# Eight-layer post-norm network on one core: weights requested a layer ahead, merged blocks around the 4-bit layer and the group norm, four-slot projections

## The chip, the core and the metric

The kernel runs on one core of a Trainium2 chip. The core has five engines with a queue of instructions each: TensorE (PE: matmuls, with PEld for its weight loads), VectorE (DVE), ScalarE (ACT), GpSimd (POOL) and SyncE (SP, which here only issues DMA transfers). They meet through semaphores. The metric is the time of one execution on the device in microseconds (us), the median of several.

## The reference

A batch of 1024 tokens with 256 features passes eight layers. After each layer the input is added and the sum is normalised (no scale or shift):

```
x = layernorm(x + linear_attention(x))        # 16 heads of 16
x = layernorm(x + golden_experts(x))          # 8 experts, 2 of them with low-rank additions
x = layernorm(x + grouped_attention(x))       # gqa: 16 query heads of 128, 4 groups
x = layernorm(x + top8_of_32_experts(x))
x = layernorm(x + latent_attention(x))        # mla: low-rank q, k, v, rotary part
x = layernorm(x + four_bit_ffn(x))            # q4
x = layernorm(x + differential_attention(x))  # diff: 16 heads of 128
x = layernorm(x + ternary_ffn(x))             # tern: weights rounded to -1, 0, 1
```

The two layers whose arithmetic the change rearranges:

```
dequant4bit(q, scale) = (q.astype(float32) - 7.5) * repeat(scale, 64, axis=1)
four_bit_ffn:  w_up = dequant4bit(w_up_q, w_up_scale).T
  y1 = x @ w_up + b_up + x @ up_lora_a @ up_lora_b;  x2 = relu(y1)
  y2 = x2 @ w_down + b_down + x2 @ down_lora_a @ down_lora_b
differential_attention, after the heads:
  out = (out - mu) * rsqrt(var + eps)               # over the 128 features of a head
  out = (out * gw + gb) * (1 - 0.8);  return out.reshape(b, s, 2048) @ Wo
```

## The kernel before

**Precision and products.** A float32 product is made of three fp32r matmuls: each operand is split in a high part (ACT copies it with rounding) and a low part (operand minus high part), and `product3` (lines L99, L100, L101) adds hi*hi, lo*hi and hi*lo. The activations are split once per layer into `x_hi` and `x_lo` by the closing of the layer before; weights are split where they are used, the low part often on POOL.

**Blocks.** A layer consists of one or two blocks. In a block each engine has its own program, in the order in which it is written; nothing is scheduled. At a block's end all engines meet in a barrier, so nothing of the next block, its DMA requests on SP among it, begins earlier. There is no work in flight across the boundary.

**`finish_layer`** (fin0, fin2, fin4, fin5, fin6, fin7, by the layer's number) projects an attention's or feed-forward's result back to 256 features and closes the layer. The contraction has `nk` chunks of 128 (2, 16, 2, 8, 16, 6), for eight tiles of 128 tokens. For a chunk ACT makes `h_hi` (128x1024, L289) and then `w_hi` (128x256, L291), DVE makes `h_lo` (L278), POOL makes `w_lo` (L266), and PE runs 8 tiles x 3 matmuls of 256 columns. There are two slots for the four split tiles, and the middle chunks run in a hardware loop (`in_pairs`); a slot is free again when PE signals `used`. The last two chunks are run tile by tile, so that the accumulators are finished one after the other. In fin7 the weights are exact in one part, and a chunk is 8 x 2 matmuls (L237, L238). Then `Closing` runs: DVE adds the residual (L139) and takes statistics, ACT takes the root, both normalise half of the tiles each, PE transposes (L200, 16), and ACT and DVE make `x_hi` and `x_lo`.

**The starts of the layers.** The first block of each layer lets SP request all its weights. golden requests the router, `temperature` and `before`, then experts and twelve low-rank pieces; gqa requests group 0, and POOL splits it (L1086, L1089) before PE may begin; mla requests 13 pieces (L1505 is the first PE use) while DVE clears the zero-padded `v_pad` (L1683, L1686) ahead of its copies L1691 and L1693 of PE's transposed weights; diff requests heads 0 and 1, then the lambda vectors and the group norm's rows, and POOL splits (L1961, L1963); tern requests `w1` to `w3`, and DVE sums `w1` (L2396).

**q4** dequantises both weights on DVE (centre L1813, scale L1816), then PE makes `up` in four parts (per part one matmul of 16x512 at L1838 and four at L1840; the trace has two records for each) and `down` in four (L1848, L1850), adding the low-rank product; 16 jobs of six matmuls of 512 columns (unit of 128 features x half of the tokens) follow. POOL adds `b_down` to `x_tok` (L1805).

**diff_norm** is a block after diff: statistics, then per head six tiles are normalised on DVE (L2290) and two on ACT (L2324), PE transposes them (L2308), and ACT applies the norm's weight and bias while it copies them to `feat` (L2335). fin6 follows with 16 chunks.

## Time and profile before

| | us |
|---|---|
| median of 3 runs (lowest to highest) | 1868.95 (1864.26 to 1869.68) |
| the profiled execution | 1871.95 |
| its span, first to last instruction | 1870.2 |
| PE busy (9441 matmuls) | 1581.6, 85% |
| DVE, ACT, POOL busy | 1041.8, 878.2, 395.5 |
| mean granted TensorE clock | 0.915 |

A matmul's busy time in the trace is longer than its distance to the next one, because matmuls are pipelined; costs are read from start to start. A row of the timeline gives the start, the duration, the engine, the line, what is written and read, and in brackets how long the engine had been idle and what ended it. DVE 56%, ACT 47% and POOL 21% are averages over stages that differ.

### The profile page before, as it was taken

What the parts mean: (1) busy time and instruction counts of PE and PEld (TensorE: products, weight loads), DVE (VectorE), ACT (ScalarE), POOL (GpSimd) and SP (SyncE); (2) the same over time, 40 slices, a digit from 0 to 9 for tenths busy, and PEclk for the clock granted to TensorE, in tenths of its full rate; (3) what the DMA queues carried; (4) which work ended last, traced back from release to release, by engine and by line L of the source; (5) the groups of instructions that cost most, each with busy time, mean ns of one, the idle gap of its engine ahead of it and who ended that gap; (6) DMA issues with size and microseconds to landing.
All of it is one profiled execution on the core that took longest, in us unless ns stands there. A gap on an engine that the chain in (4) does not pass through costs nothing. (4 is left out here: it accounts for less than half of the span.)

```text
span 1870.2 us, 27151 instructions
## 1 busy us (share of the span) xinstructions
PE 1581.6 (85%) x9441; PEld 1288.6 (69%) x9441; DVE 1041.8 (56%) x2034; ACT 878.2 (47%) x1895; POOL 395.5 (21%) x377
## 2 busy tenths in 40 slices
PE   7589959999989789995688669679999999985866
PEld 6468846766769668884466446658888888874855
DVE  3554535365363534445477640457877888766354
ACT  3343324444453333333466413346666666658433
POOL 0034531011004054542735000301101100000400
PEclk9789979999999799997799867899999999988968
DMA  1151120000000353311345020000000000001010
GB/s 55 40 154 46 46 62 18 17 0 17 0 0 0 105 136 102 90 46 30 55 59 65 5 52 0 21 13 15 18 17 8 17 17 8 9 1 45 0 47 23
DMA packets 76092, 68.12 MB, mean 36 GB/s; under 512 B 32176, under 2 KB 67208, under 8 KB 76016
## 3 DMA queue, kind: packets, MB, share of 16 engines
q1 hardware_dynamic: 71312, 62.73, 12.6%
q0 software_dynamic: 4704, 4.40, 1.9%
q8 instruction: 44, 0.72, 0.2%
q14 instruction: 32, 0.26, 0.0%
HBM read 56.46 MB, written 1.21 MB: 31 GB/s over the span
## 5 line engine op out<-in xcount | busy, mean ns | idle before, releaser
L2115 ACT ACTIVATE diff_att_probs<-psum,diff_att_neg_max 128x512 f32<-128x512 f32 x256 | 174.7, 697 | 26.9 <-DVE diff_att_neg_max L2177 26.9
L2177 DVE TENSOR_REDUCE diff_att_neg_max<-psum 128x2 f32<-128x1024 f32 x128 | 153.1, 1217 | 24.3 <-PE psum L2015 24.3
L99 PE MATMUL psum<-fin_w_hi,fin_h_hi 128*128 128x256 f32 x352 | 108.7, 309 | 45.2 <-POOL fin_w_lo L266 45.2
L2036 PE MATMUL psum<-diff_att_v_tok,diff_att_mixed_t 128*128 128x128 f32 x1024 | 127.5, 279 | 0.8 <-ACT diff_att_mixed_t L2121 0.8
L2036 PEld LDWEIGHTS psum<-diff_att_v_tok,diff_att_mixed_t 128*128 128x128 f32 x1024 | 124.2, 195 | 4.4 <-issue 1.8
L99 PEld LDWEIGHTS psum<-fin_w_hi,fin_h_hi 128*128 128x128 f32 x352 | 74.9, 213 | 49.4 <-DVE fin_h_lo L278 49.4
L100 PE MATMUL psum<-fin_w_lo,fin_h_hi 128*128 128x256 f32 x352 | 106.4, 302 | 0.0
L101 PE MATMUL psum<-fin_w_hi,fin_h_lo 128*128 128x256 f32 x352 | 106.0, 301 | 0.0
L1175 ACT ACTIVATE gqa_probs<-psum,gqa_neg_max 128x128 f32<-128x128 f32 (+3 forms) x128 | 66.5, 525 | 70.7 <-DVE gqa_neg_max L1207 70.7
L1207 DVE TENSOR_REDUCE gqa_neg_max<-psum 128x1 f32<-128x128 f32 (+3 forms) x128 | 53.8, 482 | 82.3 <-PE psum L1125 81.2
L689 POOL TENSOR_TENSOR top_scaled<-top_scaled,top_wb 128x512 f32<-128x512 f32 x48 | 65.7, 1374 | 137.2 <-DVE top_scaled L668 87.4
L1961 POOL TENSOR_TENSOR diff_att_w_hi<-diff_att_w,diff_att_zeros 128x512 fp32r<-128x512 f32 x16 | 20.6, 1287 | 348.3 <-DMA diff_att_w<-in_L_attn_Wv 348.3
L2189 DVE SCALAR_TENSOR_TENSOR diff_att_mixed<-diff_att_probs,diff_att_ratio 128x512 f32<-128x512 f32 x128 | 87.7, 747 | 1.1
L1470 POOL DMA_DIRECT2D mla_att_q_own<-mla_att_parts x144 | 71.3, 504 | 55.0 <-PE psum L1572 50.8
L1135 PE MATMUL psum<-gqa_probs_t,gqa_v_tok 128*128 128x512 f32 (+3 forms) x256 | 76.4, 441 | 6.8 <-DVE gqa_probs_t L1230 6.8
L668 DVE TENSOR_TENSOR top_scaled<-top_gate,psum 128x512 f32<-128x512 f32 x48 | 32.9, 687 | 87.0 <-PE psum L101 65.1
L1122 PE MATMUL psum<-gqa_k_feat,gqa_q_feat 128*128 128x128 f32 (+3 forms) x256 | 78.6, 451 | 3.1 <-ACT gqa_q_feat L1165 3.1
L646 ACT ACTIVATE top_gate<-psum 128x512 f32<-128x512 f32 x48 | 28.6, 598 | 108.5 <-PE psum L101 108.5
L2022 PE MATMUL psum<-ident,diff_att_mixed 128*128 128x128 f32 x512 | 70.8, 282 | 8.7 <-DVE diff_att_mixed L2189 7.0
L1667 ACT ACTIVATE mla_att_probs<-psum,mla_att_neg_max 128x128 f32<-128x128 f32 (+3 forms) x128 | 65.8, 528 | 26.2 <-DVE mla_att_neg_max L1719 25.6
L99 PE MATMUL psum<-x_hi,top_w_hi 128*128 128x512 f32 x192 | 76.5, 399 | 0.0
L100 PE MATMUL psum<-x_lo,top_w_hi 128*128 128x512 f32 x192 | 76.2, 397 | 0.0
(435 smaller groups left out, 4482.1 us busy)
## 6 DMA issues: line engine op xcount, KB each, us to landing
top_wb<-top_w_dram SPq DMA_DIRECT2D x16, 384.0 KB, 4.1
golden_wb<-golden_w_dram SPq DMA_DIRECT2D x8, 512.0 KB, 4.2
top_wb<-top_w_dram SPq DMA_DIRECT2D x16, 256.0 KB, 4.0
mla_att_k_feat<-mla_att_parts SPq DMA_DIRECT2D x56, 64.0 KB, 4.4
mla_att_q_own<-mla_att_parts POOLq DMA_DIRECT2D x112, 32.0 KB, 3.5
top_w_nat<-in_L_ffn_w SPq DMA_DIRECT2D x16, 192.0 KB, 3.0
top_w_nat<-in_L_ffn_v SPq DMA_DIRECT2D x16, 192.0 KB, 4.2
top_down_w<-in_L_ffn_w SPq DMA_DIRECT2D x1, 3072.0 KB, 13.5
```

The lines of the kernel that those rows point to most:

```text
L99: nc.tensor.matmul(out, s_hi, m_hi, start=start, stop=False)
L100: nc.tensor.matmul(out, s_hi, m_lo, start=False, stop=False)
L101: return nc.tensor.matmul(out, s_lo, m_hi, start=False, stop=stop)
L1122: nc.tensor.matmul(bank[qt][:, 0:(qt + 1) * P], q_feat[:, h, b * SEQ + qt * P:b * SEQ + (qt + 1) * P], k_feat[:, b * SEQ:b * SEQ + (qt + 1 ...
L1135: last = nc.tensor.matmul(bank[6][:, kt * P:SEQ], v_tok[:, b * QT + kt, :], probs_t[:, kt, 0:SEQ - kt * P], start=kt == 0, stop=kt == QT - 1)
L1175: nc.scalar.activation(probs[:, u % 2, qt, 0:(qt + 1) * P], bank[qt][:, 0:(qt + 1) * P], ACT.Exp, bias=neg_max[:, u % 2, qt:qt + 1], accum ...
L1470: eng.dma_start(q_own[to:to + 8, p % 2, j, cols].bitcast(F32), parts[at_row:at_row + 8, 1, kind, Q_PARTS[part], cols].bitcast(F32)).then_i ...
L2022: last = nc.tensor.transpose(bank[4 + kt % 2][:, qt * P:(qt + 1) * P], mixed[:, u % 2, qt, kt * P:(kt + 1) * P], ident[:])
L2036: last = nc.tensor.matmul(bank[6][:, qt * P:(qt + 1) * P], mixed_t[:, u % 2, kt, qt * P:(qt + 1) * P], v_tok[:, slot, b * QT + kt, :], sta ...
L2115: last = nc.scalar.activation(probs[:, qt, m, :], bank[2 * (qt % 2) + m], ACT.Exp, bias=neg_max[:, qt, m:m + 1], accum_out=row_sum[:, qt, ...
L2177: nc.vector.tensor_reduce(neg_max[:, qt, :], psum[:, 2 * (qt % 2):2 * (qt % 2) + 2, :], AX.X, ALU.max, negate=True).then_inc(maxed, 1)
L2189: last = nc.vector.scalar_tensor_tensor(mixed[:, u % 2, qt, :], probs[:, qt, 1, :], ratio[:, qt:qt + 1], probs[:, qt, 0, :], ALU.mult, ALU ...
```

## The change

1. **Ahead.** New `Prefetch` classes hold tiles (`ahead...`) on the right side of the memory that outlive the block. A layer gets `pre` (its own) and `nxt` (of the layer after): SP requests the next layer's first weights behind its own, and POOL splits gqa's group 0 at the end of golden's program and diff's heads 0 and 1 at the end of q4's. golden, gqa, top8, mla, diff and tern (here from within diff_norm) are served so. The lambda vectors and `v_pad`'s clearing stay in the layer.
2. **`finish_layer`**: up to four slots, no loop, `w_hi` ahead of `h_hi`, and `h_hi`, `h_lo` in two halves of 512 columns.
3. **q4** and fin4 share a block, `q4_up`: fin4's projection, the small transposes, up parts 0 and 1, the closing's transposes, then the 16 jobs with up parts 2 and 3 ahead of the fifth job, down parts ahead of the ninth and the twelfth. The centring is on ACT, the scaling on POOL.
4. **diff_norm** and fin6 share a block: the norm's weight is multiplied into `wo` (ACT for `w_hi`; POOL two instructions per head for `w_scaled` and `w_lo`), its bias is summed over the heads into one row (DVE) and added by 16 matmuls with ones; PE transposes a head, ACT and DVE split it from PSUM, and the head's product follows at once. DVE normalises five tiles per head, ACT three. `wo` is loaded in diff.

```diff
-def finish_layer(nc, env, name, nk, hidden, w, out=None, exact_w=False, whole=True):
+def finish_layer(nc, env, name, nk, hidden, w, out=None, exact_w=False, whole=True, nxt=None):
+    SLOTS = min(nk, 4)
-        w_hi, w_lo = (st.sb(f"w_{n}", [P, 2, D], F32R) for n in ("hi", "lo"))
+            w_hi, w_lo = (st.sb(f"w_{n}", [P, SLOTS, D], F32R) for n in ("hi", "lo"))
...
+            for k in range(nk):
+                wait_slot(act, k)
+                if not exact_w:
+                    nc.scalar.activation(w_hi[:, k % SLOTS], w[:, k, :], ACT.Copy).then_inc(w_high, 1)
+                for half in range(2):
+                    nc.scalar.activation(h_hi[:, k % SLOTS, half_cols(half)], hidden[:, k, half_cols(half)], ACT.Copy).then_inc(h_high, 1)
...
+class Prefetch:
+    def place(self, top):
+        nc.sbuf_top = top
+        self.t = {n: nc.alloc_sbuf_tensor(f"{self.name}_{n}", shape, dt, side="right") for n, (shape, dt) in self.SHAPES.items()}
...
+PREFETCH = [None, GoldenPrefetch, GroupedPrefetch, TopPrefetch, LatentPrefetch, LatentContext, DifferentialPrefetch, TernaryPrefetch]
...
 # golden, POOL
             ge.pool_program(pool, down_chunk, wb_wait)
+            if nxt:
+                nxt.split(pool)
...
 # q4_up, PE after fin4's projection and the small transposes
+                up_part(0)
+                up_part(1)
+                close.tensor(pe)
+                for j, (hc, half) in enumerate(jobs):
+                    if j == UP_SECOND:
+                        up_part(2)
+                        up_part(3)
+                    if j == DOWN_FIRST:
+                        pe.wait_ge(dequantised, 2)
+                        down_part(0)
+                        down_part(1)
+                    if j == DOWN_SECOND:
...
 # diff_norm, POOL, PE and DVE per head
+                for h in range(HEADS):
+                    pool.wait_ge(w_high, h + 1)
+                    nc.gpsimd.tensor_tensor(w_scaled[:, h % 2], wo[:, h], gn[:, 0, h:h + 1].to_broadcast([P, D]), ALU.mult).then_inc(w_multiplied, 1)
+                    pool.wait_ge(w_multiplied, h + 1)
+                    nc.gpsimd.tensor_tensor(w_lo[:, h], w_scaled[:, h % 2], w_hi[:, h].bitcast(F32), ALU.subtract).then_inc(w_split, 1)
...
+                for h in range(HEADS):
+                    if h + 1 < HEADS:
+                        transposes(h + 1)
+                    pe.wait_ge(h_low, 2 * h + 2)
+                    pe.wait_ge(w_split, h + 1)
+                    if h < HEADS - 2:
+                        for t in range(NT):
+                            last = product(h, t)
```

On POOL, at the end of golden and the start of gqa, before the change (the ISA row belongs to the barrier):

```order
L630 TENSOR_TENSOR golden_d_lo<-golden_down_w,golden_d_hi 128x256 x3
L77 UNCONDITIONAL_BRANCH
L2524 ISA
L1078 UNCONDITIONAL_BRANCH
L1080 MEMSET gqa_zeros 128x1024
L1086 TENSOR_TENSOR gqa_wk_hi<-gqa_wk_g,gqa_zeros 128x256
L1086 TENSOR_TENSOR gqa_wq_hi<-gqa_wq_g,gqa_zeros 128x1024
L1089 TENSOR_TENSOR gqa_wk_lo<-gqa_wk_g,gqa_wk_hi 128x256
L1089 TENSOR_TENSOR gqa_wq_lo<-gqa_wq_g,gqa_wq_hi 128x1024
```

and with it:

```order
L819 TENSOR_TENSOR golden_d_lo<-golden_down_w,golden_d_hi 128x256 x3
L378 MEMSET ahead_zeros 128x1
L383 TENSOR_TENSOR ahead_wk_hi<-ahead_wk_g,ahead_zeros 128x256
L383 TENSOR_TENSOR ahead_wq_hi<-ahead_wq_g,ahead_zeros 128x1024
L386 TENSOR_TENSOR ahead_wk_lo<-ahead_wk_g,ahead_wk_hi 128x256
L386 TENSOR_TENSOR ahead_wq_lo<-ahead_wq_g,ahead_wq_hi 128x1024
L77 UNCONDITIONAL_BRANCH
L2818 ISA
L1247 UNCONDITIONAL_BRANCH
```

The four splits of group 0 have moved from behind the barrier to in front of it; they stand behind the last scalings and splits of golden.

On PE in the 4-bit layer, before (L1838 and L1840 make the up weight; the down parts and then the jobs follow):

```order
L1827 MATMUL psum<-ident,q_up_a 16x128 x2
L1828 MATMUL psum<-ident,q_b_rows 128x8
L1830 MATMUL psum<-ident,q_down_a 16x128 x8
L1838 MATMUL psum<-q_up_b,q_up_at 128x512
L1840 MATMUL psum<-ident,q_up_nat 128x128 x4
L1838 MATMUL psum<-q_up_b,q_up_at 128x512
L1840 MATMUL psum<-ident,q_up_nat 128x128 x4
L1838 MATMUL psum<-q_up_b,q_up_at 128x512
L1840 MATMUL psum<-ident,q_up_nat 128x128 x4
L1838 MATMUL psum<-q_up_b,q_up_at 128x512
L1840 MATMUL psum<-ident,q_up_nat 128x128 x4
L1848 MATMUL psum<-q_down_b,q_down_at 128x256
```

and with the change (L1975 and L1977 make the up weight, L202 is fin4's closing, L99 to L101 the first job):

```order
L2008 MATMUL psum<-ident,q_up_b_rows 128x8
L2010 MATMUL psum<-ident,q_up_down_a 16x128 x8
L1975 MATMUL psum<-q_up_up_b,q_up_up_at 128x512
L1977 MATMUL psum<-ident,q_up_up_nat 128x128 x4
L1975 MATMUL psum<-q_up_up_b,q_up_up_at 128x512
L1977 MATMUL psum<-ident,q_up_up_nat 128x128 x4
L202 MATMUL psum<-ident,x_tok 128x128 x16
L99 MATMUL psum<-x_hi,q_up_up_hi 128x512
L100 MATMUL psum<-x_lo,q_up_up_hi 128x512
L101 MATMUL psum<-x_hi,q_up_up_lo 128x512
```

Two of the up parts stand between the projection and the closing's transposes, and the first job no longer waits for the other parts, which stand between later jobs.

## Rows read from the trace of the kernel before

**Rows 1.** Waits of TensorE, whole span: who waited for whom; total us, times, longest.

```profile
PE psum L99 <- POOL fin_w_lo L266: 45.2, 22, 9.9
...
PE psum L99 <- POOL gqa_wq_lo L1089: 14.8, 1, 14.8
PE psum L1505 <- DMA mla_att_o_nat<-in_L_attn_W_o: 12.5, 1, 12.5
PE psum L1827 <- DMA q_b_down<-in_L_ffn_b_down: 12.4, 1, 12.4
...
PE psum L2433 <- DVE tern_row_sum L2396: 10.1, 1, 10.1
PE psum L99 <- POOL diff_att_w_lo L1963: 9.8, 1, 9.8
...
PE psum L862 <- DMA golden_before<-in_const_before: 6.9, 1, 6.9
```

**Rows 2.** Timeline of TensorE in fin2: start, us, instruction [idle before <-releaser].

```profile
563.07 0.41 PE L101 MATMUL psum<-fin_w_hi,fin_h_lo 128*128 128x256 f32 x1
563.28 0.41 PE L99 MATMUL psum<-fin_w_hi,fin_h_hi 128*128 128x256 f32 x1
```

**Rows 3.** The same, end of fin2's matmuls.

```profile
618.60 0.28 PE L100 MATMUL psum<-fin_w_lo,fin_h_hi 128*128 128x256 f32 x1
618.72 0.28 PE L101 MATMUL psum<-fin_w_hi,fin_h_lo 128*128 128x256 f32 x1
```

**Rows 4.** Windows, TensorE alone: stretch, us, busy (count), PEclk, DMA share, GB/s.

```profile
561.00:619.00 58.00, 51.83 (x384) 0.91 0.00 0
1072.90:1162.30 89.40, 72.58 (x259) 0.67 0.11 28
1103.60:1137.80 34.20, 34.14 (x88) 0.50 0.00 0
1141.80:1162.30 20.50, 20.49 (x88) 1.00 0.00 1
1166.30:1197.40 31.10, 26.69 (x192) 0.90 0.00 1
1691.50:1786.40 94.90, 74.27 (x512) 0.89 0.03 8
```

**Rows 5.** Timeline of GpSimd, start of gqa.

```profile
267.30 0.95 POOL L1080 MEMSET gqa_zeros<- 128x1024 f32 x1 [19.08 <-POOLq L2524]
...
275.59 0.72 POOL L1089 TENSOR_TENSOR gqa_wk_lo<-gqa_wk_g,gqa_wk_hi 128x256 fp32r<-128x256 f32 x1
```

**Rows 6.** Timeline at the start of mla.

```profile
871.68 6.88 DVE L1683 MEMSET mla_att_v_pad<- 128x8192 f32 x1 [2.72 <-issue]
...
882.72 0.69 DVE L1693 COPY mla_wo_t<-psum 128x512 f32<-128x512 f32 x1 [0.91 <-PE psum L1517]
...
885.95 1.45 PE L1534 MATMUL psum<-x_feat,mla_att_w_t 128*128 128x512 f32 x3
```

**Rows 7.** Timeline at the start of diff.

```profile
1211.67 0.43 SPq L1948 DMA_DIRECT2D diff_att_lam_in<-in_L_attn_lambda_k  x1
...
1215.53 0.57 DVE L2234 TENSOR_TENSOR diff_att_lam_prod<-diff_att_lam_in 128x128 f32<-128x128 f32 x1 [9.15 <-DMA diff_att_lam_in<-in_L_attn_lambda_k]
...
1217.99 2.05 PE L1999 MATMUL psum<-diff_att_w,x_feat 128*128 128x128 f32 x16 [1.57 <-DVE diff_att_k_lo L2167]
```

**Rows 8.** Line L266 (POOL, fin_w_lo): duration ns min/median/max, first and last start.

```profile
L266 POOL TENSOR_TENSOR fin_w_lo<-gqa_w_dense,fin_w_hi x16: 1457/1486/1709, 559.4 to 608.9; 128x256 fp32r<-128x256 f32 x16
```

**Rows 9.** Timeline around the 4-bit layer's weight making.

```profile
1099.93 4.59 POOL L1805 TENSOR_TENSOR x_tok<-x_tok,q_b_down 128x2048 f32<-128x2048 f32 x1 [27.18 <-DMA q_b_down<-in_L_ffn_b_down]
...
1102.87 2.74 DVE L1813 TENSOR_SCALAR q_down_nat<-q_down_q 128x2048 f32<-128x2048 int32 x1 [2.71 <-DMA q_down_scale<-in_L_ffn_w_down_scale]
```

**Rows 10.** Lines of diff_norm and fin6: line, count, busy, mean ns, idle before.

```profile
L2290 DVE TENSOR_SCALAR diff_ctx_tok<-diff_ctx_tok,diff_norm_mean,diff_norm_var 128x128 f32<-128x128 f32 x96 | 24.7, 338 | 0.0
...
L2308 PE MATMUL psum<-ident,diff_ctx_tok 128*128 128x128 f32 x128 | 21.7, 310 | 14.3 <-ACT diff_norm_feat L2335 7.7 <-DVE diff_ctx_tok L2290 6.2
```

More of the change, by code:

```diff
@@ L1750, in _, with four_bit_ffn @@
                 context(PAIRS - 1)
-        finish_layer(nc, env, "fin4", DC, ctx, wo_t, out=env.out if env.last == 5 else None, whole=False)
-def four_bit_ffn(nc, env):
+def four_bit_ffn(nc, env, pre, nxt):
     bank, x_tok, ident, src = env.bank, env.x_tok, env.ident, env.src
@@ L1790, in _ @@
+            close = Closing(nc, env, "fin4", up, None, False, acc, lambda eng, t: eng.wait_ge(projected, t // 2 + 1), first_bank=4)
+            block = up.block()
+            flat = lambda a: a[:].rearrange("p c d -> p (c d)")
+            up_parts = [(0, 0), (1, 0), (0, 1), (1, 1)]
+            jobs = [(hc, half) for hh in range(2) for half in range(2) for hc in range(4 * hh, 4 * hh + 4)]
+            UP_SECOND, DOWN_FIRST, DOWN_SECOND = 4, 8, 11
             @block.sync
@@ L1823, in _ @@
+                pool.wait_ge(bias_loaded, 16)
+                pool.wait_ge(close.transposed, 4)
+                nc.gpsimd.tensor_tensor(x_tok[:], x_tok[:], b_down[:].unsqueeze(1).to_broadcast([P, NT, D]), ALU.add).then_inc(biased, 1)
+                if nxt:
+                    nxt.split(pool)
             @block.tensor
             def _(pe):
-                pe.wait_ge(small_loaded, 6 * 16)
-                for c in range(DC):
-                    nc.tensor.transpose(bank[4][0:R, c * P:(c + 1) * P], up_a[:, c, :], ident[:])
```

751 lines of the change are left out of this document (478 added, 273 removed).

## The prediction

> **What bounds the kernel now.** I read the page first, then TensorE's waits, then the timeline at each of them, then windows. PE is busy 1581.6 of 1870.2 us, more than any other engine, so it is the clock of the kernel, and a stage gets shorter where PE's idle time or its half-speed time does. The waits of PE [rows 1] name both kinds of gap that the change is about: 45.2 us in 22 waits for POOL's `fin_w_lo`, all in projections, and single waits of 14.8, 12.5, 12.4, 10.1, 9.8 and 6.9 us at the starts of gqa, mla, q4, tern, diff and golden. The second kind of cost is half speed. In fin2, two matmuls of 256 columns start 0.21 us apart early on [rows 2] and 0.12 us apart at the end [rows 3]: the two levels, 1.2 and 2.4 GHz. The window of q4's weight making [rows 4] has the granted clock at 0.50 for all of its 34.20 us, although PE is busy 34.14 of them; the jobs behind it run at 1.00.
>
> **Starts of layers.** A start does not gain its whole wait; what is late next takes over.
> - gqa: the requests and all four splits go. The splits (the fourth and longest ends at 278.6, the third took 0.72 us) move to the end of golden, where POOL has nothing more to do while the closing runs, some 18 us. PE may begin as the block does, about when POOL's clearing at 267.30 does now [rows 5]. The wait of 14.8 us [rows 1] had begun 3.4 us ahead of that and keeps this part, the barrier's: **11.2** (8 to 12).
> - golden: the router waits 6.9 us for `before` [rows 1], and a low-rank piece costs a second wait. PE's own work moves up by 7.6, but the first scaled expert needs the routing weights, which go through ACT, DVE and a round trip to memory whose length doesn't change. I take **5.3** (3 to 8).
> - mla: the wait is 12.5, but DVE clears `v_pad` first, 6.88 us from 871.68, and only then copies the transposed weights; PE's matmul at 885.95 waits for the copy at 882.72 [rows 6]. None of this DVE work moves: without the requests it still ends at about 880.8, and the copies then find their transposes waiting. PE resumes at 882.35 instead of 885.95, gain 3.6, less about 1.1 for matmuls that find the clock low after the gap: **2.5** (0 to 9.3; the upper end if another engine's work covers it).
> - diff: POOL's 9.8 goes, but the lambda vectors stay. Their last request ends at 1212.10 before and about 2.6 us earlier now, as six requests are gone ahead of them; DVE's product at 1215.53 and two small steps lie between them and the matmul at 1217.99 [rows 7]. So the queue's shift sets it: **2.9** (1 to 6.2).
> - tern: 10.1 goes as a request, DVE's clearings (until 1796.8) are next, and the sum starts there instead of 1800.3: **3.5** (2 to 6). top8: its router's request and transposes **1.7**. Together 27.1.
>
> **Projections.** In fin2, 384 matmuls take 58.0 us [rows 4]. At 0.12 us from start to start [rows 3] they are 46.1, and 1.6 more for a first part at 0.21 [rows 2] makes 47.7. What covers the rest: with four slots, ACT (0.40 + 2 x 0.6 us), DVE (2 x 0.7) and POOL stay ahead of 2.88 us of PE per chunk. POOL's 1.49 us per chunk [rows 8] is the longest of them, and it fits even so. The start comes 1.0 sooner, since `w_hi` no longer stands behind 1.06 us of `h_hi`. fin2: 10.3 + 1.0 = **11.3** (8 to 12). fin5, 192 matmuls in 31.1 us [rows 4], becomes 23.0 + 1.6: 6.5 + 1.0 = **7.5** (5 to 8). fin7, by the same count with two matmuls per tile, **5.5** (4 to 7; its closing is DVE's and does not shrink). fin0 **1.0**. Together 25.3.
>
> **fin4 and q4.** Before, from the first projection matmul to the last job, 89.4 us pass, of them 72.6 busy at a mean clock of 0.67 [rows 4]. Now: the projection 7.9, small transposes 2.7 and a wait of about 1 for the dequantised weight (requested with the block's start, some 4 us behind it centred, then POOL's 4.59 us for 128x2048, the price of L1805 [rows 9]); two up parts, which at half speed cost 4.0 each (the 34.20 us of rows 4 are four of these and four down parts of 4.6); closing's transposes and `x_hi`, `x_lo` to the first job at 27 us from the start. Then 16 jobs of 6 x 0.233 = 22.4, 2 up parts and 4 down parts. If these run at full speed between jobs they are 4.2 and 9.2; I add 2 for a slow beginning and 5 for three short falls of the clock, 43 in all. 27 + 43 = 70 against 89.4: **19.5**. If every part costs the half-speed price worked out from rows 4 (8.0 and 18.4), 13.0 more, less the 5 already counted: 11.5. If nothing falls and no wait appears, 27. Range 10 to 27.
>
> **The group norm and fin6.** Before, 94.9 us from the first transpose to the last projection matmul, 512 matmuls [rows 4]. Now one pass: per head 24 matmuls x 0.12 = 2.88 and 8 transposes. A transpose costs 21.7/128 = 0.17 before [rows 10] with half of them slow, or 0.12 close-packed; I take 1.1 per head, so 4.0. DVE has 5 x 24.7/96 = 1.3 [rows 10], two low parts of 0.69, a 128x256 step of 0.4: 3.1. POOL has two steps of 0.72 [rows 5]: 1.5. ACT 2.9. PE is the longest. The transposes of two heads and the split of one stand ahead of the first product, which starts 4.4 us after the first transpose at 1691.5, so at 1695.9. From there 384 x 0.12 = 46.1, the other 14 heads' transposes 15.4, 16 shift matmuls 1.9 and 1.5 for a slow beginning: 64.9, which ends at 1760.8; before it was 1786.3. Less 0.3 for a closing that reads two tiles per bank: **25.2** (15 to 31).
>
> The sum: 27.1 + 25.3 + 19.5 + 25.2 = 97.1. The profiled execution took 1871.95, so it would be 1774.9; the median of the runs shown is 3.0 below that execution, which gives 1772.
>
> **A rule weighed against the rows.** A split of 128x256 takes POOL 0.72 us in gqa, where DVE rests [rows 5], and a median of 1.486 in fin2, where DVE works beside it [rows 8]; L1813 on DVE took 2.74 us beside the long POOL step [rows 9]. The Trainium skill (SBUF — State Buffer, section "SBUF: two separate sides") says that VectorE and GpSimd hold a shared port pair exclusively for a whole instruction, and that VectorE wants it in a two-port mode or with two SBUF inputs. By that rule fin6's low part, now read from PSUM, would leave POOL alone and only the 0.4 us step would block: the price per head stays PE's 4.0. The rows don't show such a step alone; they only show the doubling. What they allow at worst is rival B.
>
> **Rivals.**
> - A (0.15): q4's parts stay at half speed wherever they stand. For it: 34 us of nearly unbroken work didn't raise the clock [rows 4]. Against: jobs lie between them now, and jobs raised it. q4 gains 11.5: 1780. The Trainium skill (TensorE: Matmul & The Clock Gate, section "What's actually happening") says that the throttled state is the default and that activity releases it; this trace does not agree, with 34.14 us busy at 0.50 [rows 4]. By that rule the parts would run at full speed, which is q4's upper end: 1765.
> - B (0.12): in the fused norm DVE and POOL exclude each other fully: 3.1 + 1.5 = 4.6 per head, 0.6 x 16 = 10 more. 1782. For: the doubling above. Against: half of DVE's steps read PSUM.
> - C (0.12): the start gaps go whole (mla 9.3, diff 6.2, golden 7.6, tern 6): 15 more, 1757. Against: the DVE and SP chains of rows 6 and 7.
> - D (0.02), the other side: TensorE falls to 1.2 GHz in the unrolled projections and stays there. Each of 384 + 192 + 384 + 96 = 1056 matmuls would cost 0.213 in place of 0.120 us: 98 us, and the norm's 128 transposes, now between them, 11 more. Together 109 against 97 gained: 1881. It decides once nine tenths of this work run so. For it: q4's weight making did [rows 4]. Against: fin2 had 0.91 granted over its 58 us, gaps included [rows 4], and fp32r matmuls of 256 columns at 0.12 apart [rows 3].
>
> My forecast holds 0.58, and 0.01 is left for what no row shows. With A and B together 1790, with small losses 1797; with C and a norm at its best 1750: range 1750 to 1798. Runs of this kernel spread by 0.3%, which is what I count as no change; the forecast lies 5% away, so only D and that rest are not faster: 0.97, 0.01, 0.02.
>
> **What would show it.** PE's first matmul of gqa at the block's start; mla's first rotary matmul still behind L1832's copy; fin2's 384 matmuls in 48 us and no wait for `fin_w_lo` beyond the first; PE and not DVE the engine without gaps in the norm, 4.0 us per head; the granted clock in q4_up above 0.8 from the first job on. The prediction is wrong if a projection's chunks take more than 3.2 us, if PE waits in the norm in every head, or if q4_up from projection to last job takes over 80.

## The result, and the profile after

The changed kernel takes 1761.84 us (median of 4 runs, 1761.27 to 1769.47), against 1867.87 us for the kernel before (4 runs, 1864.26 to 1869.68): a ratio of 0.9444, 95% interval 0.9414 to 0.9474. The forecast was 1772 (1750 to 1798). The profiled execution took 1761.27 us. Its span is 1759.4 us, 110.8 shorter than the 1870.2 before; 97.1 were forecast.

This is the head of the page of the kernel after:

```profile
span 1759.4 us, 26913 instructions
...
PE 1551.3 (88%) x9465; PEld 1268.7 (72%) x9465; DVE 1048.7 (60%) x2079; ACT 870.1 (49%) x1931; POOL 377.2 (21%) x399
...
PEclk9789989999999899998889988799999999997978
```

By the trace's records TensorE executes 24 matmuls more than before and is busy 30.3 us less. The work did not shrink: more of it ran at the upper clock level (mean granted clock 0.936 against 0.915). If a busy microsecond at the lower level is counted as half, PE's work is 1477.7 us before and 1475.1 after (worked out from the two traces). The other 80.5 us are time in which PE stood idle before. PE is still the busiest engine over the span (88%), with DVE at 60%; in the group norm both are full, as shown below.

The gain by stage, with the time of each counted from the last PE instruction of the stage in front to its own last one; fin0 counts from the start of the span and the last row to its end (worked out from PE's timelines):

| stage | before | after | gained | forecast |
|---|---|---|---|---|
| fin0 | 80.4 | 78.7 | 1.7 | 1.0 |
| golden | 183.5 | 178.5 | 5.0 | 5.3 |
| gqa | 293.1 | 276.8 | 16.3 | 11.2 |
| fin2 | 68.0 | 56.7 | 11.3 | 11.3 |
| top8 | 241.6 | 238.9 | 2.7 | 1.7 |
| mla | 196.4 | 192.7 | 3.7 | 2.5 |
| fin4 and q4 | 99.3 | 69.9 | 29.4 | 19.5 |
| fin5 | 41.4 | 35.3 | 6.1 | 7.5 |
| diff | 480.0 | 478.6 | 1.4 | 2.9 |
| norm and fin6 | 108.5 | 84.5 | 23.9 | 25.2 |
| tern and fin7 | 78.0 | 68.8 | 9.3 | 9.0 |

The waits of TensorE after, which answer to [rows 1] (columns as there):

```profile
PE psum L99 <- PEq L2818: 7.5, 2, 3.9
...
PE psum L2195 <- DVE diff_att_k_lo L2363: 6.4, 3, 4.4
PE psum L2716 <- DVE tern_row_sum L2679: 6.4, 1, 6.4
PE psum L99 <- DVE fin_h_lo L283: 6.2, 2, 3.2
...
PE psum L2558 <- DVE diff_ctx_tok L2494: 4.5, 1, 4.5
...
PE psum L99 <- POOL fin_w_lo L274: 3.9, 1, 3.9
...
PE psum L1645 <- PEq L2818: 3.4, 1, 3.4
...
PE psum L99 <- DVE q_up_up_lo L2095: 3.1, 1, 3.1
```

Of the six starts in [rows 1] only tern's wait keeps its releaser, at 6.4 instead of 10.1 us. L2818 is the barrier that starts a block: five layers now begin behind it after 3.4 to 3.9 us (the 7.5 are gqa's 3.9 and diff's 3.6). The 22 waits for `fin_w_lo` have become one, at the start of fin0; where fin2 starts, PE now waits 2.9 us for DVE's `fin_h_lo` instead (its row has 6.2 us in two waits). The wait in diff has grown from 1.6 to 4.4 us, and one of 3.1 in q4 is new.

Windows after, TensorE alone, columns as in [rows 4], whose stretches they answer: fin2; fin4 and q4 from the first projection matmul to the last job; three pieces of that stretch; fin5; the group norm with fin6.

```profile
536.90:584.80 47.90, 47.79 (x384) 0.96 0.00 1
1032.80:1092.30 59.50, 55.11 (x259) 0.91 0.16 37
1040.00:1049.00 9.00, 7.82 (x51) 1.00 0.27 74
1052.00:1056.00 4.00, 3.94 (x12) 0.67 0.02 4
1073.00:1077.00 4.00, 4.00 (x14) 0.60 0.00 0
1095.40:1121.30 25.90, 25.75 (x192) 0.89 0.00 1
1615.00:1683.90 68.90, 65.66 (x528) 0.94 0.03 10
```

fin2's 384 matmuls went from 58.00 to 47.90 us and hold almost no idle time (0.11 us). The q4 stretch went from 89.4 to 59.5, at 0.91 instead of 0.67. In fin2, in q4 and in the norm with fin6 both kinds of cost shrank, the gaps and the half-speed part; neither is gone in all three (0.96, 0.91 and 0.94 granted).

### The profile page after: what moved, and what is told of

The parts are those of the page before. It is cut to its first block and busy times, and to the rows that moved or that the text cites. A ratio compares the mean times of both kernels' runs of the same rounds, so it can differ in the third digit from the quotient of the medians.

```text
span 1759.4 us, 26913 instructions
## 1 busy us (share of the span) xinstructions
PE 1551.3 (88%) x9465; PEld 1268.7 (72%) x9465; DVE 1048.7 (60%) x2079; ACT 870.1 (49%) x1931; POOL 377.2 (21%) x399
## 5 line engine op out<-in xcount | busy, mean ns | idle before, releaser
L1332 ACT ACTIVATE gqa_att_probs<-psum,gqa_att_neg_max 128x128 f32<-128x128 f32 (+3 forms) x128 | 66.5, 525 | 65.3 <-DVE gqa_att_neg_max L1364 65.3
L459 POOL TENSOR_TENSOR ahead_w_hi<-ahead_w,ahead_zeros 128x512 fp32r<-128x512 f32 x16 | 16.7, 1041 | 377.1 <-DMA ahead_w<-in_L_attn_Wv 377.0
L1364 DVE TENSOR_REDUCE gqa_att_neg_max<-psum 128x1 f32<-128x128 f32 (+3 forms) x128 | 53.8, 482 | 69.0 <-PE psum L1282 67.9
L1292 PE MATMUL psum<-gqa_att_probs_t,gqa_att_v_tok 128*128 128x512 f32 (+3 forms) x256 | 76.4, 441 | 6.8 <-DVE gqa_att_probs_t L1387 6.8
L1279 PE MATMUL psum<-gqa_att_k_feat,gqa_att_q_feat 128*128 128x128 f32 (+3 forms) x256 | 76.1, 440 | 3.1 <-ACT gqa_att_q_feat L1322 3.1
L99 PE MATMUL psum<-x_hi,top_w_hi 128*128 128x512 f32 x192 | 77.0, 401 | 0.0
L101 PE MATMUL psum<-x_hi,top_w_lo 128*128 128x512 f32 x192 | 76.4, 398 | 0.0
L2317 ACT ACTIVATE diff_att_mixed_t<-psum 128x512 f32<-128x512 f32 x128 | 70.9, 624 | 7.1 <-PE psum L2218 7.0
L2195 PE MATMUL psum<-ahead_w,x_feat 128*128 128x128 f32 x512 | 67.2, 286 | 6.4 <-DVE diff_att_k_lo L2363 6.4
L99 PE MATMUL psum<-fin_w_hi,fin_h_hi 128*128 128x256 f32 x208 | 62.4, 300 | 10.1 <-DVE fin_h_lo L283 6.2
```

The source lines that it names most:

```text
L99: nc.tensor.matmul(out, s_hi, m_hi, start=start, stop=False)
L101: return nc.tensor.matmul(out, s_lo, m_hi, start=False, stop=stop)
L1279: nc.tensor.matmul(bank[qt][:, 0:(qt + 1) * P], q_feat[:, h, b * SEQ + qt * P:b * SEQ + (qt + 1) * P], k_feat[:, b * SEQ:b * SEQ + (qt + 1 ...
L1292: last = nc.tensor.matmul(bank[6][:, kt * P:SEQ], v_tok[:, b * QT + kt, :], probs_t[:, kt, 0:SEQ - kt * P], start=kt == 0, stop=kt == QT - 1)
L2317: nc.scalar.activation(mixed_t[:, u % 2, kt, :], bank[4 + kt % 2], ACT.Copy).then_inc(t_read, 1)
```

## The experiments

Three groups of four kernels, in the order of their numbers, each group on a chip of its own with the kernel before run beside it. All times are medians. Times of stages are of the one profiled execution of each kernel.

| kernel | us (n) | lowest to highest | before, same chip (n) |
|---|---|---|---|
| e1_downs_together | 1767.77 (2) | 1764.23 to 1771.32 | 1864.74 (4) |
| e2_up_early | 1757.17 (2) | 1755.47 to 1758.87 | |
| e3_two_slots | 1769.79 (2) | 1769.67 to 1769.91 | |
| e4_full_zeros | 1769.77 (2) | 1768.61 to 1770.93 | |
| e5_thin_zeros_before | 1866.57 (8) | 1858.19 to 1872.20 | 1867.80 (13) |
| e6_changed_again | 1762.96 (4) | 1759.21 to 1769.34 | |
| e7_late_clear | 1757.50 (4) | 1756.92 to 1762.53 | |
| e8_lambda_ahead | 1759.58 (4) | 1757.37 to 1761.35 | |
| e9_three_together | 1753.91 (5) | 1750.67 to 1754.95 | 1867.30 (15) |
| e10_changed_third | 1764.87 (5) | 1760.95 to 1766.19 | |
| e11_gqa_own_load | 1774.90 (2) | 1773.61 to 1776.18 | |
| e12_w_first_before | 1860.62 (8) | 1854.10 to 1866.04 | |

**The changed kernel again** (e6 and e10, no edit). This sets how much a difference between two kernels means.

> The changed kernel once more, without an edit. In three variants whose code up to q4's first job is the changed kernel's, the time from fin4's first projection matmul to that job was 19.2, 23.0 and 23.0 us, and 19.2 in its own profile. Theory: TensorE's clock falls there in some executions and not in others, so the run can show either value, and executions spread by about 4 us on this account alone. Rival: the variants' edits shift it; then this run shows 19.2 again and all its executions lie within 2 us.

> The changed kernel without an edit, beside the three edits together, for the comparison on one chip. Median 1762 with executions from 1759 to 1770 by the spread seen so far.

Measured: 1762.96 and 1764.87, ratios 0.9423 (0.9401 to 0.9445) and 0.9446 (0.9423 to 0.9469). The profiled execution of e6 took 1769.34, 8 us more than that of the result. Its stages show where: gqa 280.6 against 276.8, mla 195.9 against 192.7, top8 241.1 against 238.9. Executions of one kernel spread over 10 us, and not in one place, so a single total says nothing about an edit of 3 us; a stage or a wait may. The rival's 2 us are out. But q4's first stretch took 19.3 us in e6 and 19.2 in e10, the value of after: no profiled execution of the kernel without an edit had the other value, so the theory's half, that one kernel shows both, is not shown.

**q4: down parts together** (e1). Four down parts in a row ahead of the ninth job, instead of two and two.

```diff
-            UP_SECOND, DOWN_FIRST, DOWN_SECOND = 4, 8, 11
+            UP_SECOND, DOWN_FIRST, DOWN_SECOND = 4, 8, 8
```

> The changed kernel with all four down parts of q4 ahead of the ninth job, in place of two there and two ahead of the twelfth. Theory: the weight-making parts don't hold TensorE's clock; in the changed kernel they run at full speed (2.5 us each) because they start at full speed and are short enough, and the clock falls only once, after two of them. Then the third and fourth part, following on directly, cost half-speed prices (4.6 to 5 instead of 2.5 us each), and the stretch from q4's first job to its last grows from 40.2 to 42.5 to 45 us. Rival: the parts ran at half speed in the kernel before only because TensorE came out of a 12.4 us wait; once at full speed they keep it. Then the stretch stays within 0.5 us of 40.2.

Measured: the jobs' stretch, from the first job to the last one's end, took 45.9 us, against 40.2 in the profiled execution after. The timeline of TensorE in e1 (start, us; L1985 and L1987 make a down weight):

```profile
1075.55 0.69 PE L1985 MATMUL psum<-q_up_down_b,q_up_down_at 16*128 16x256 f32 x2
1076.17 0.71 PE L1987 MATMUL psum<-ident,q_up_down_nat 128*128 128x128 f32 x4
...
1079.97 1.03 PE L1987 MATMUL psum<-ident,q_up_down_nat 128*128 128x128 f32 x4
1080.93 1.22 PE L1985 MATMUL psum<-q_up_down_b,q_up_down_at 16*128 16x256 f32 x2
```

and a window of e1 over the later down parts:

```profile
1080.00:1092.00 12.00, 12.00 (x34) 0.51 0.00 0
```

TensorE comes from jobs at the upper level and makes the first two down weights at 0.69 and 0.71 us a piece. In the next row the same piece takes 1.22, with no gap in front. It was busy for all 12.00 us of the last window, and the granted clock was 0.51. So four down parts in a row don't keep the clock even when it starts high. From the first down part to the last job e1 takes 27.6 us and after 23.0; this 4.6 is the edit's price, within the 2.3 to 4.8 of the theory. The other 1.1 us of the 45.9 come from a first stretch at the lower level, which e4 and e7 have without this edit (41.3 us for the jobs' stretch). Two down parts in a row lose the clock only at their end, in the kernel after between 1073 and 1077 us (0.60), and in e9 and e11 not at all: there the same part of the stage takes 21.4 us.

**q4: up parts early** (e2). All four up parts ahead of the jobs; ACT reads all four.

```diff
-            UP_SECOND, DOWN_FIRST, DOWN_SECOND = 4, 8, 11
+            UP_SECOND, DOWN_FIRST, DOWN_SECOND = 0, 8, 11
...
                 read_up(1)
+                if UP_SECOND == 0:
+                    read_up(2)
+                    read_up(3)
```

> The changed kernel with up parts 2 and 3 ahead of q4's first job, in place of ahead of the fifth; they fill the wait of 3.1 us for up_lo. Theory (parts don't hold the clock): four up parts with the closing's transposes make over 8 us of such work, the clock falls before the first jobs; the gain of 3.1 us from the filled wait is mostly lost again, from the last projection matmul to the last job 52.1 us become 50 to 53. Rival (only waits lower the clock): the wait is filled and with it the fall behind it (1.7 us) goes, 47 to 48 us.

Measured: from the last projection matmul to the last job 50.5 us. The same stretch takes 52.2 after, in e6 and in e10, and 56.4 in e4 and e7. e2's first stretch ran at the lower level, as in e4 and e7, so 56.4 is the fair neighbour: 5.9 better. The wait of 3.1 us for `q_up_up_lo` is what the two parts fill, and the fall of the clock behind it is gone too. So 50.5 lies in the theory's range only because of the lower level in front. The same edit at the upper level (e9) takes 45.7, or 6.5 less than 52.2, which is the rival's gain and more: four up parts, with the closing's transposes between the second and the third, kept the clock there.

```profile
1039.10:1049.20 10.10, 10.08 (x55) 1.00 0.03 7
```

**Two slots** (e3). Everything else of the unrolled projection stays.

```diff
-    SLOTS = min(nk, 4)
+    SLOTS = 2
```

> The changed kernel with two slots in place of four in every projection of finish_layer, everything else unrolled as it is. Theory: the four slots carry most of what fin2 and fin5 gained: fin2 from its first to its last matmul grows from about 47.5 by 6 to 10 us, fin5 by 3 to 5. Rival: the halves of 512 columns and w_hi ahead of h_hi carry it, and two slots are enough: fin2 grows by less than 2 us.

Measured: fin2 59.1 (after: 56.7), fin5 37.5 (35.3), tern and fin7 70.8 (68.8). Of TensorE's waits in fin2 of e3 this one is new:

```profile
PE psum L99 <- POOL fin_w_lo L274: 1.3, 1, 1.3
```

One wait for POOL returns, ahead of the last two chunks. The third and fourth slot are worth 2.4 of fin2's 11.3 us; my theory wanted 6 to 10 from them and falls, and the rival's bound of 2 is missed by a little (unedited, fin2 took 56.0 to 57.1). The two slots with unrolling, `w_hi` first and the halves already hold 8.9.

**The order within the old loop** (e12). The kernel before, with ACT making `w_hi` ahead of `h_hi`, POOL waiting for the first and DVE for the second of the two.

```diff
-                nc.scalar.activation(h_hi[:, slot:slot + 1], hidden[:, ds(k), :], ACT.Copy).then_inc(high_made, 1)
                 if not exact_w:
                     nc.scalar.activation(w_hi[:, slot:slot + 1], w[:, ds(k), :], ACT.Copy).then_inc(high_made, 1)
+                nc.scalar.activation(h_hi[:, slot:slot + 1], hidden[:, ds(k), :], ACT.Copy).then_inc(high_made, 1)
```

> The kernel before with one edit: in every projection ACT makes a chunk's w_hi ahead of its h_hi; two slots and the loop stay. Theory: PE's waits in fin2 (0.5 us in each of six loop passes, 3.1 at the loop's exit, and 3.4 us of half speed behind that) come from w_lo, which stands behind 1.06 us of h_hi; with w_hi first the six waits go, the exit wait shrinks to about 2 or less with no fall behind it, the start comes 1.0 sooner: fin2 68.0 to 58 to 61. Rival: the two slots set it, since a slot is free only when PE has done with the chunk two before; fin2 65 to 67.

Measured: 1860.62, ratio 0.9961 (0.9945 to 0.9978); fin2 65.0 (before: 68.0). TensorE's waits in fin2 of e12:

```profile
PE psum L99 <- DVE fin_h_lo L278: 6.6, 2, 3.7
```

The six waits of 0.5 us for POOL, one in each pass of the loop, are gone. What is left is the start and a wait of 2.9 us as the loop is left, now for DVE instead of POOL. The kernels' text says what this second wait is: PE takes the last two chunks tile by tile and needs both split before it starts, and the last one's slot comes free only with the chunk two before. e3, without a loop, still has it, at 1.3 us. The order did more than move a wait, as POOL's step in fin2 of e12 shows (compare [rows 8]):

```profile
L266 POOL TENSOR_TENSOR fin_w_lo<-gqa_w_dense,fin_w_hi x16: 725/742/1461, 554.9 to 601.8; 128x256 fp32r<-128x256 f32 x16
```

With `w_hi` first POOL works while ACT still makes `h_hi`, and so before DVE's step: its median falls from 1.486 to 0.742 us. fin2's 65.0 lies in the rival's range, but its reason, the two slots, is not what e3 shows. So of fin2's 11.3 us about 3.0 are the order, 2.4 the slots, and the rest, some 6, the unrolling together with the halves. I worked this last part out as the remainder; no kernel had either alone.

**gqa: the prefetch alone** (e11). Group 0 is requested and split in gqa's own block again; all else stays.

```diff
-            if nxt:
-                nxt.load(sp)
...
-            if nxt:
-                nxt.split(pool)
...
+                pre.load(sp, 0)
...
+                pre.split(pool, 0)
```

> The changed kernel with gqa's group 0 requested and split in gqa's own block again. Theory (the whole 11.2 us at the start come from this part alone): PE's first matmul comes 14 to 15 us after golden's last transposes instead of 3.9, gqa 286.5 to 292 against 276.5 to 280.6, and golden's time does not change beyond the 175.7 to 178.5 seen, since the split there was hidden. Rival: the four POOL operations at golden's end slow DVE's closing by the shared port; then golden is 1 to 2 us shorter than 175.7.

Measured: 1774.90 against 1764.87 of e10, both on one chip. The start of gqa in e11:

```profile
269.60 0.80 PE L99 MATMUL psum<-x_hi,ahead_wk_hi 128*128 128x512 f32 x1 [14.14 <-POOL ahead_wq_lo L386]
```

The wait of 14.8 us is back as 14.1, instead of the 3.9 after; gqa takes 290.4 us (276.4 to 280.6 in the kernels with the prefetch), and golden stays at 176.8. So the prefetch's gain in gqa is the wait, 10.3 us, and POOL's splits cost nothing that golden's time shows (175.6 to 178.6 in the other kernels with the prefetch). The rest of e11's difference, 276.2 us behind gqa's first matmul against 272.9, comes with a fall of the clock in group 0 that the profile after doesn't have.

**gqa: POOL's operand of zeros** (e4 and e5). The change also made `zeros` one column, read as broadcast. e4 gives the changed kernel the full tile back; e5 gives the kernel before the one column.

```diff
-"zeros": ([P, 1, 1], F32)}
+"zeros": ([P, DC, HPG * HD], F32)}
...
-t["zeros"][:].to_broadcast([P, DC, raw.shape[2]])
+t["zeros"][:, :, 0:raw.shape[2]]
```

> The changed kernel with gqa's zeros for POOL's split as a full 128x1024 tile, as before, in place of one column read again and again. Theory: the broadcast column makes POOL's two additions 0.57 us shorter per group (1.89 and 0.61 us against 2.34 and 0.72), DVE's normalisation of the probabilities behind it ends sooner, PE's wait there shrinks from 2.6 to 1.9 us, and with it the fall of TensorE's clock after that wait goes (0.59 granted over the next 4 us before, 1.00 now). With the full tile the wait and the fall come back in three groups: gqa grows by 4 to 6 us, 276.8 to 281 to 283. Rival: the clock's falls come from where the block starts in time; gqa grows by at most 2.1 us (three times the 0.7 of the wait).

> The kernel before with one edit: gqa's zeros for POOL's split are one column, read again and again. Theory: POOL's additions are 0.57 us shorter per group, PE's waits of 2.55 and 2.76 us in the second and third group become about 2.1, and at that length the clock stays up (1.00 in the four us behind them, 0.59 and 0.67 before): gqa 293.1 to 288 to 289.5. Rival: the falls have nothing to do with the wait's length; only 0.5 us per group goes, gqa 291.5 to 292.5.

Measured: with the full tile gqa takes 277.9 (276.8 after), with waits of 2.4 us instead of 1.9 and no fall of the clock behind them. With the one column the kernel before takes 290.5 in gqa (293.1) and 0.9991 (0.9971 to 1.0012) of its time, which is no change. The waits of TensorE in two of gqa's groups in e4:

```profile
PE psum L1196 <- DVE gqa_att_probs L1374: 4.8, 2, 2.4
```

After, the same row has 3.8 in 2, the longest 1.9. The shorter wait is due to the operand; it moves 0.5 us a time. The falls that I had hung on it don't come back with it, so e4 speaks for the rival: gqa grew by 1.1 us. e5 lies between the two ranges and decides nothing.

**mla: the clearing behind the copies** (e7). The same instructions in another order on DVE; the clearing of the last columns goes with it.

```diff
-                nc.vector.memset(v_pad[:], 0.0).then_inc(v_filled, 1)
...
                 nc.vector.tensor_copy(wo_t[:].rearrange("p c e -> p (c e)"), bank[3]).then_inc(w_read_dve, 1)
+                nc.vector.memset(v_pad[:], 0.0).then_inc(v_filled, 1)
```

> The changed kernel with mla's clearing of v_pad behind DVE's copies of the transposed weights and not ahead of them. Theory (the clearing is what is late once the requests are gone): PE's wait of 4.5 us ahead of the rotary matmuls goes; a wait of up to 2 us may come where DVE applies the tables later. mla 192.7 to 188.5 to 190.5. Rival (something else ends just behind it, or the clearing delays the tables as much): mla within 1 us of 192.7.

Measured: 1757.50, 5.5 us less than e6 on the same chip; mla 187.8 us (192.7 after; 195.9 in e6 and 192.8 in e8, which ran on the same chip with this stage unedited). The timeline at mla's start, after, which answers to [rows 6]:

```profile
834.77 6.88 DVE L1822 MEMSET mla_att_v_pad<- 128x8192 f32 x1 [2.75 <-issue]
...
844.68 0.68 DVE L1832 COPY ahead_wo_t<-psum 128x512 f32<-128x512 f32 x1
...
845.51 1.19 PE L1674 MATMUL psum<-x_feat,mla_att_w_t 128*128 128x512 f32 x1 [4.52 <-DVE ahead_wo_t L1832]
```

and in e7:

```profile
840.07 6.88 DVE L1828 MEMSET mla_att_v_pad<- 128x8192 f32 x1 [1.65 <-issue]
...
841.92 1.45 PE L1674 MATMUL psum<-x_feat,mla_att_w_t 128*128 128x512 f32 x3
```

TensorE goes into L1674 with no wait at all, and the 6.88 us of clearing lie beside its work. The wait was DVE's, as the prediction had it.

**diff: the lambda vectors ahead** (e8). Their requests move to q4's block, with a tile and a semaphore that outlive it.

```diff
+        for i, n in enumerate(("q1", "k1", "q2", "k2")):
+            sp.dma_start(self.t["lam_in"][:, i], self.env.src[f"L3_attn_lambda_{n}"].partition_broadcast(P)).then_inc(self.sem["lam_loaded"], 16)
...
-            lam_in = at.sb("lam_in", [P, 4, DH])
+            lam_in = pre.t["lam_in"]
```

> The changed kernel with the four lambda vectors requested in q4's block, behind the weights of heads 0 and 1. Theory (their landing is what is late in diff): ACT reaches k_hi when the first projection's bank is ready, PE's wait of 4.4 us ahead of the k and v matmuls shrinks to under 1.5, and the fall of the clock behind it goes too: diff 478.6 to 474 to 475.5. Rival: ACT's table load and the DVE steps hold k_hi as long; diff falls by less than 1.5 us.

Measured: 1759.58, 3.4 us less than e6 on the same chip; diff 474.7 us (478.6 after). After, DVE's product of the vectors, behind which its low part of k stands, which the v matmuls wait for:

```profile
1136.24 0.29 DVE L2430 TENSOR_TENSOR diff_att_lam_prod<-diff_att_lam_in 128x128 f32<-128x128 f32 x1 [6.30 <-DMA diff_att_lam_in<-in_L_attn_lambda_k]
```

and in e8:

```profile
1131.11 0.29 DVE L2430 TENSOR_TENSOR diff_att_lam_prod<-ahead_lam_in 128x128 f32<-128x128 f32 x1 [1.07 <-PEq L2818]
...
1135.64 1.65 PE L2195 MATMUL psum<-ahead_w,x_feat 128*128 128x128 f32 x6 [1.49 <-DVE diff_att_k_lo L2363]
```

The product comes 5.1 us sooner and PE's wait falls from 4.4 to 1.5. The wait is shown; the stage's 3.9 us are less sure, since the unedited diff took 478.3 to 479.4 us in eight kernels and 475.7 in a ninth (e11).

**The three together** (e9: the edits of e2, e7 and e8).

> The changed kernel with three edits at once: mla's clearing behind the copies, the lambda vectors requested in q4's block, and q4's up parts 2 and 3 ahead of the first job. Theory: they lie in three stages and add up. From the stages measured so far: mla 187.8 (4.9 to 8.1 less), diff 474.7 (3.9 less), fin4 and q4 68.9 (1.0 less than the changed kernel's better value, 5.9 less than its worse one). Together 10 to 14 us under the changed kernel of the same call, about 1750. Rival: the mixture of clock falls moves with every edit and eats part of it; under 7 us.

Measured: 1753.91 us (5 runs), ratio to before 0.9388 (0.9366 to 0.9410), and 11.0 us less than the changed kernel on the same chip (e10). It is the fastest of all. The windows of q4 and of diff's first 40 us in e9:

```profile
1029.00:1082.10 53.10, 51.75 (x259) 0.97 0.19 45
1118.90:1158.90 40.00, 30.89 (x117) 0.63 0.21 63
```

q4's stretch is 53.1 us, 6.4 less than after. diff's start ran at 0.63, and the stage took 480.6: in that execution the clock took back what the earlier vectors gave. The 11.0 us lie in the theory's 10 to 14, but not as its sum. Against the profiled execution of e10, mla gained 3.2, fin4 and q4 6.5, diff lost 2.0, and top8, which no edit touched, took 4.3 less (239.0 against 243.3). That the clock moves with every edit, as the rival had it, is seen; that it leaves under 7 us is not.

## Why the prediction was right, and where its sizes were off

Most mechanisms came as forecast: starts that gain up to the second wait, chunks without gaps, a norm bound by PE. The one in the projections did not, as said under fin2, though its number did. The 97.1 us became 110.8, and two terms hold the difference: q4 with 9.9 and gqa with 5.1, together 15.0; the others cancel to 1.3 the other way.

**q4 (forecast 19.5, measured 29.4).** The step that failed is the size of 'two up parts, which at half speed cost 4.0 each' and '5 for three short falls of the clock'. The forecast was 27 us to the first job and 43 behind it; the trace has 19.2 and 40.2. Of the 7.8 us in front, the two up parts hold 3.8 (4.2 for 8.0), the closing's transposes and splits 2.4, the small transposes 1.2 and the projection 0.6, less 0.2 for the wait. TensorE in q4's first stretch, after:

```profile
1042.87 1.12 PE L1975 MATMUL psum<-q_up_up_b,q_up_up_at 16*128 16x512 f32 x2 [1.15 <-ACT q_up_down_at L2065]
1043.92 1.16 PE L1977 MATMUL psum<-ident,q_up_up_nat 128*128 128x128 f32 x8
1045.01 1.12 PE L1975 MATMUL psum<-q_up_up_b,q_up_up_at 16*128 16x512 f32 x2
...
1052.06 0.50 PE L99 MATMUL psum<-x_hi,q_up_up_hi 128*128 128x512 f32 x1 [3.09 <-DVE q_up_up_lo L2095]
```

and in e7, which differs in mla alone:

```profile
1039.72 1.12 PE L1975 MATMUL psum<-q_up_up_b,q_up_up_at 16*128 16x512 f32 x2 [1.15 <-ACT q_up_down_at L2065]
1040.77 1.99 PE L1977 MATMUL psum<-ident,q_up_up_nat 128*128 128x128 f32 x8
1042.69 2.07 PE L1975 MATMUL psum<-q_up_up_b,q_up_up_at 16*128 16x512 f32 x2
```

The instructions and the wait of 1.15 us ahead of them are the same. After, an up part takes 2.14 us from start to start; in e7 its second half is at the lower level already and the next part takes 4.0. The stage then takes 69.9 or 74.9 us (72.2 in e11, which has no fall among the jobs' down parts). I had the lower level as certain because all 34.20 us before had it [rows 4]. The profiled executions of e1, e2, e4, e7 and e11 had it there, those of after, e3, e6, e8, e9 and e10 not. All five are kernels with an edit somewhere, so the runs don't tell whether an edit's shift in time or the execution decides. The window of e7 from projection to last job, a stretch that took 59.50 us at 0.91 in e10:

```profile
1029.00:1093.40 64.40, 60.18 (x259) 0.83 0.14 35
```

With the lower level, as in e7, my forecast of 19.5 is 4.9 too low, with the upper one 9.9. The upper level in the profiled execution is luck that the forecast had no part in. In neither case do the parts among the jobs behave as rival A had it. The jobs' stretch had two falls, one after two down parts and one behind the wait of 3.1 us, not three. That rival's mechanism, parts that lower the clock wherever they stand, is not wholly wrong all the same: e1 shows it with four down parts in a row. e9's up parts, at 1.00 for 10.10 us, show the opposite, so what lowers the clock is open. The Trainium skill (TensorE: Matmul & The Clock Gate, section "What's actually happening") has activity release the throttle; e1's 12.00 busy us at 0.51, entered from the upper level, do not agree with it.

**gqa (11.2, 16.3).** The start came as forecast: the wait went from 14.8 to 3.9, and e11 confirms 10.3. The other 5 are inside the groups, where I had put nothing. After, the two waits for DVE's normalised probabilities are 1.9 us each (2.56 and 2.77 before, with a third of 1.05), and no window behind them shows a fall; before, two did. These are the waits and the granted clock before:

```profile
PE psum L1015 <- DVE gqa_probs L1217: 6.4, 3, 2.8
```

```profile
380.00:384.00 4.00, 3.86 (x16) 0.59 0.00 0
451.00:455.00 4.00, 3.64 (x16) 0.67 0.00 0
```

Counted from gqa's first matmul, the stage went from 278.3 to 272.9 us. e4, with the full tile and no fall, takes 274.2, so POOL's shorter addition (below) is worth up to 1.3 of the 5.4, and the two falls that stayed away the larger part. A shorter wait is not what keeps the clock up. e12, the old kernel with another edit, has the same wait of 2.56 us and no fall behind it:

```profile
380.30:384.30 4.00, 3.97 (x23) 1.00 0.00 0
```

and in e6 a wait of 2.19 us is followed by one, in e3 a wait of 2.19 us is not. Unedited, gqa took 276.8, 277.3 and 280.6. So most of the 5 us is where the clock falls in an execution, which the forecast could not have, and which another execution takes back.

**fin2, fin5, fin7 (11.3, 7.5 and 5.5; measured 11.3, 6.1 and about 5.8).** fin2 has its forecast to the tenth, and 384 matmuls in 47.9 against the 47.7 I worked out. The credit was wrongly given, though, so the agreement is luck in its cause. I said that four slots cover POOL's 1.49 us and that this is the longest of the producers' steps; by my own figures ACT's 0.40 + 2 x 0.6 is longer, and POOL's step is no longer 1.49. Its median is 0.746 us in fin2 after, as in e12, because of the order. e3 shows two slots to be nearly enough, e12 that the order took 3.0. The largest part, some 6, is the unrolling with the halves, which no kernel separates; the wait ahead of the last two chunks, 3.1 us before, 2.9 in e12 and 1.3 in e3, and the half speed behind it belong to it. For fin7 the 5.8 is the stage's 9.3 less the 3.5 forecast for tern, whose wait fell from 10.1 to 6.4, or 3.7. fin5's window ran at 0.89, a longer beginning at half speed than the 1.6 us allowed.

**mla (2.5, 3.7) and golden (5.3, 5.0).** mla as worked out: its matmul still stands behind the copy at L1832, comes 3.5 us sooner (3.6 forecast), and e7 takes that wait away; the 1.1 us for a low clock were not paid in this execution, but mla took up to 195.9 us in others. golden agrees in this execution, where it took 178.5; in others it took as little as 175.6, a gain of 7.9, so 5.3 and rival C's 7.6 are not told apart. Rival C, that the gaps go whole, is out for mla (4.5 us remain), diff (4.4 us) and tern (6.4 us).

**diff (2.9, 1.4).** The v matmuls start 3.4 us sooner, counted from the closing (10.9 instead of 14.3). The window of the first 40 us from PE's first matmul of the stage, before and then after:

```profile
1213.50:1253.50 40.00, 29.33 (x157) 0.91 0.05 12
```

```profile
1131.00:1171.00 40.00, 26.65 (x128) 0.82 0.22 67
```

The lower clock there took about 2 back. The term was right and the clock behind it not foreseen.

**The norm and fin6 (25.2, 23.9).** From the first product to the last matmul 63.8 us for 16 heads, or 3.99 a head; the forecast was 4.0. That agreement hides two errors: in the middle the heads start 3.74 us apart, as 8 transposes take 0.87 and not the 1.1 taken, and the ends cost more. It lost 1.8 us at the start, which waits 4.5 us for DVE's first normalised tiles. PE hardly waits afterwards (65.66 busy of 68.90). Rival B needed DVE and POOL to exclude each other. The groups of GpSimd after, between 1620 and 1684 us:

```profile
L2536 POOL TENSOR_TENSOR diff_norm_w_lo<-diff_norm_w_scaled,diff_norm_w_hi 128x256 fp32r<-128x256 f32 x13 | 9.8, 752 | 1.0
L2534 POOL TENSOR_TENSOR diff_norm_w_scaled<-diff_wo,diff_gn 128x256 f32<-128x256 f32 x12 | 7.5, 628 | 28.5 <-ACT diff_norm_w_hi L2596 28.5
```

The steps take 0.75 and 0.63 us beside a busy DVE, where a split took 1.49 in fin2 [rows 8], so B's 4.6 us a head are refuted. By the Trainium skill (SBUF — State Buffer, section "SBUF: two separate sides") DVE needs the shared pair with two SBUF inputs or in a two-port mode, and its low part here has only one input in SBUF; for this step the trace agrees (0.68 us beside POOL and alone). But B's mechanism is there on the other side. DVE's normalising step, which I counted at 24.7/96 = 0.26 whatever POOL does, is the one that stretches; its row (ns min/median/max), then the busy time of all engines (PE, PEld, DVE, ACT, POOL) between 1624 and 1664 us:

```profile
L2494 DVE TENSOR_SCALAR diff_ctx_tok<-diff_ctx_tok,diff_norm_mean,diff_norm_var x80: 329/337/891, 1612.4 to 1666.7; 128x128 f32<-128x128 f32 x80
```

```profile
1624.00:1664.00 40.00, 40.00 (x345) 40.00 (x344) 39.17 (x86) 27.71 (x64) 13.44 (x20) 1.00 0.01 1
```

The 40 of these steps that meet a step of POOL have a median of 0.65 us, the 40 others 0.34 (worked out from the timeline). The step that the prediction expected to block, DVE's at L2501, takes 0.47 us in the three cases that meet a step of POOL and in the others. DVE is busy 39.17 of 40.00 us, or 3.7 a head where 3.1 was forecast: PE sets the pace, with its matmuls 0.12 us apart, but DVE has almost nothing left, so by these busy times faster matmuls alone would gain 2% there at most (an estimate).

**Rival D**, half speed throughout the unrolled projections, is out: fin2 had 0.96.

What stays open: what decides whether q4's first stretch has the upper level, and why four down parts lose it where four up parts keep it; how fin2's 6 us divide between the unrolling and the halves; and the exact split of gqa's 5 us. The gains of q4's merged block and of the fused norm, 29.4 and 23.9 us, rest on the windows before and after; no kernel here takes either of them back alone.

## What to carry to other kernels

A start that waits for a load is worth only the distance to whatever stands second, so name that second wait and move it in the same step: a clearing behind the copies and four small requests in an earlier block gave 5 and 4 us in their stages here, each in a kernel of its own. When one engine feeds another through a rotating buffer, look first at the order of the producer's steps, which also decides which engines work at the same moment, and at the wait ahead of the last chunks; more slots came last. Don't read a few tenths of a per cent from one execution: compare stages and waits, and run the unedited kernel beside each trial.

## What the runs showed of the hardware that was not expected

- GpSimd adds faster when its second operand is one column broadcast. The row of after (min, median, max in ns), for an addition of 128x1024 and of 128x256:

```profile
L383 POOL TENSOR_TENSOR ahead_wk_hi<-ahead_wk_g,ahead_zeros x4: 614/615/682, 241.6 to 423.8; 128x256 fp32r<-128x256 f32 x4
L383 POOL TENSOR_TENSOR ahead_wq_hi<-ahead_wq_g,ahead_zeros x4: 1893/1894/2005, 242.2 to 424.4; 128x1024 fp32r<-128x1024 f32 x4
```

  With the full tile the same additions took 2.35 and 0.73 us before.
- Two engines that work on SBUF at once can cost either of them: POOL's split of 128x256 takes 1.486 us (median) beside DVE's two-input step in fin2 before and 0.742 in e12, where it is mostly over before DVE's begins; DVE's 128x128 normalising step takes 0.34 us by itself and 0.65 when it meets a step of POOL.
- TensorE busy without a gap may sit at its lower level: 12.00 of 12.00 us at 0.51 in e1, after it had come from the upper one. It need not: four up parts and 16 transposes ran at 1.00 for 10.10 us in e9.
- The same instructions got either level in the executions of kernels that differ elsewhere, 2.1 or 4.0 us a part in q4. And equal waits are followed by either: 2.56 us by 0.59 before and by 1.00 in e12.
- Between the last transposes of a layer and the first instruction of TensorE in the next block 3.4 to 3.9 us pass at five starts after (up to 4.2 in other executions), and no edit here touched it. The barrier is the smaller part. Ahead of gqa's first matmul, at 261.08, DVE still makes `x_lo` until 259.62:

```profile
258.15 1.47 DVE L166 TENSOR_TENSOR x_lo<-x_feat,x_hi 128x512 fp32r<-128x512 f32 x2
```

  From the end of that step 1.5 us are left here, and 0.9 to 1.2 at the other four starts.
